# Row maxima turned by VectorE and stored through DRAM, expert gathers spread over steps, a third sum buffer, the first stack loaded in two parts

## The reference, cut to what matters

```python
scores = jnp.einsum('bhqd,bhkd->bhqk', q, k) * scale + bias   # 16 heads of 16, causal, 2048 x 2048
attn = jax.nn.softmax(scores, axis=-1)
out = jnp.einsum('bhqk,bhkd->bhqd', attn, v)
...
xs = xf[tok]                                   # 1024 tokens, 2 experts of 8 each, sorted by expert
h = gelu(ragged_dot(xs, w1, tokens_per_expert))
out = zeros_like(xf).at[tok].add(ragged_dot(h, w2, tokens_per_expert) * flat_w[order][:, None])
```

## Time and profile before

| | |
|---|---|
| runs, us | 4152.18, 4156.4, 4167.15; median 4156.4 |
| profiled execution: its own time, its span | 4157.57, 4155.8 |
| TensorE matmul busy | 3989.5 us, 96% |
| VectorE, ScalarE, GpSimd busy | 2997.2, 2798.6, 846.1 us |
| mean granted TensorE clock | 0.990 |

### The profile page before, as it was taken

One profiled execution on the slowest core, in us unless ns is written; L12 is line 12 of the kernel. 1 busy time (PEld: TensorE's weight loads), 2 busy tenths in 40 slices (PEclk: granted clock), 3 DMA queues, 4 the chain that ended last, 5 costly groups with the idle time before them and its releaser, 6 DMA issues.

```text
span 4155.8 us, 108094 instructions
## 1 busy us (share of the span) xinstructions
PE 3989.5 (96%) x42400; PEld 2460.7 (59%) x42401; DVE 2997.2 (72%) x4046; ACT 2798.6 (67%) x5828; POOL 846.1 (20%) x1176
## 2 busy tenths in 40 slices
PE   6999999999999999999999999999999999999998
PEld 4555555555555555557865555555555555558854
DVE  5888888887878788873038888888888878881074
ACT  2677777777777777775247777777777777773264
POOL 3100001111111123231022333333323232110020
PEclk8999999999999999999999999999999999999999
DMA  6322233324333343235553333333333333345522
GB/s 182 76 57 54 61 82 79 70 75 88 81 77 78 84 104 104 81 102 172 178 156 84 93 91 90 94 98 98 98 91 96 86 77 87 68 103 191 181 71 71
DMA packets 246892, 406.29 MB, mean 98 GB/s; under 512 B 29307, under 2 KB 161859, under 8 KB 233283
## 3 DMA queue, kind: packets, MB, share of 16 engines
q1 hardware_dynamic: 243310, 390.99, 35.8%
q0 software_dynamic: 3072, 8.39, 0.8%
HBM read 263.78 MB, written 121.21 MB: 93 GB/s over the span
## 4 chain that ended last, share of the span: by engine, by line
PE 48%; ACT 4%; DVE 3%; issue 2%; DMA 1%; SPq 0%; ACTq 0%; POOL 0%; DVEq 0%
PE ps_acc L1027 12%; PE ps_r L966 9%; PE ps_p L996 8%; PE ps_p L1137 5%; PE ps_r L1150 5%; ACT probs L848 4%; PE ps_r L1065 3%; DVE part_max L1326 2%; PE ps_r L1073 2%; PE ps_r L1069 1%; PE ps_r L971 1%; PE ps_p L990 1%; PE ps_p L1003 0%; PE ps_r L962 0%; PE ps_r L1058 0%
## 5 line engine op out<-in xcount | busy, mean ns | idle before, releaser
L1326 DVE TENSOR_REDUCE part_max<-ps_p 128x2 f32<-128x1024 f32 (+3 forms) x2560 | 2625.5, 1061 | 654.4 <-PE ps_p L996 496.4
L848 ACT ACTIVATE probs<-ps_r 128x512 f32<-128x512 f32 (+1 forms) x4608 | 2335.2, 575 | 667.0 <-PE ps_r L966 402.2
L966 PE MATMUL ps_r<-q_stack,k_stack 54*128 54x512 f32 (+3 forms) x5120 | 1381.3, 392 | 31.4 <-ACT probs L848 27.9
L996 PE MATMUL ps_p<-k_stack,q_stack 52*128 52x512 f32 (+3 forms) x5120 | 1238.2, 425 | 49.9 <-DVE part_max L1326 25.3
L1027 PE MATMUL ps_acc<-probs,v_head 128*17 128x256 f32 x19456 | 1146.1, 361 | 1.6 <-ACT probs L848 1.6
L966 PEld LDWEIGHTS ps_r<-q_stack,k_stack 54*128 54x128 f32 x5120 | 727.3, 187 | 261.7 <-ACT probs L848 212.7
L1027 PEld LDWEIGHTS ps_acc<-probs,v_head 128*17 128x17 f32 x19456 | 488.8, 97 | 463.0 <-issue 224.1
L996 PEld LDWEIGHTS ps_p<-k_stack,q_stack 52*128 52x128 f32 x5120 | 556.6, 186 | 343.3 <-issue 161.4
L1401 DVE COPY xf<-ps_r 128x256 f32<-128x256 f32 x60 | 25.5, 425 | 402.3 <-PE ps_r L1150 402.3
L911 ACT ACTIVATE hid_f<-ps_p 128x256 f32<-128x256 f32 x240 | 92.0, 383 | 301.7 <-PE ps_p L1137 301.7
L971 PE MATMUL ps_r<-id,mk 64*128 64x64 bf16 x3558 | 280.6, 194 | 0.0
(11 more groups left out here) (134 smaller groups left out, 2408.0 us busy)
## 6 DMA issues: line engine op xcount, KB each, us to landing
probs<-w_dram SPq DMA_DIRECT2D x58, 1024.0 KB, 7.1
q_stack<-parts SPq DMA_DIRECT2D x384, 128.0 KB
k_stack<-parts SPq DMA_DIRECT2D x384, 128.0 KB
parts<-pa SPq DMA_DIRECT2D x128, 256.0 KB, 2.5
parts<-pb SPq DMA_DIRECT2D x128, 256.0 KB, 3.5
o_sums<-acc_sb SPq DMA_DIRECT2D x1008, 17.0 KB
swp<-tmp SPq DMA_DIRECT2D x128, 128.0 KB
bk<-recips SPq DMA_DIRECT2D x58, 256.0 KB
```

The lines of the kernel that those rows point to most:

```text
L848: act.activation(probs[:, at % PBUF, u, 0:w], block_bank(g, n, u)[:, 0:w], ACT.Exp)\
L966: mm = pe.matmul(bank[:, col:col + QW - q0], ks[s][r, kb * P:(kb + 1) * P], qs[s][r, qt * QW + q0:(qt + 1) * QW], start=fresh, stop=True, ...
L996: mm[u] = pe.matmul(banks[:, u, col:col + w], qs[s][r, qb * P:(qb + 1) * P], ks[s][r, kc * QW:kc * QW + w], start=fresh, stop=True, skip_g ...
L1326: mm = dve.tensor_reduce(part_max[:, :, qb, kc], ps_p[:, p1_banks(g, n), col:col + w], AX_X, ALU.max)
```

## The change

1. `c` is no job of TensorE and ScalarE any more. VectorE itself transposes `cp` in blocks of 32 x 32 to `cblk`; SP stores that to DRAM (`cd`, steps 26 and 4) and loads it back, rearranged in runs of 32 numbers, into `q_stack` (`c`, steps 29 and 7).
2. `acc_sb` has three buffers in place of two.
3. The 16 gathers of an expert stage stand at steps 3, 5, 7 and so on of the next stack; the mixing starts at step 31 in place of 19.
4. Stack 0 is loaded in two parts, chunks 0 to 2 while chunk 3 is still computed; SP waits for `rows_copied` only after the first chunk's stores, and the constant rows of slots 1 and 2 come after stack 0.
5. ScalarE ends each expert stage with an exponential of one column, which loads that table there.
6. `bl` of a chunk stands 20 steps ahead of the projection in place of 16, but not before 16 steps behind the last projection of a routed chunk (2 behind another).
7. `zx` stands 5 steps behind its load `zr` in place of beside it.

```diff
-C_HI, C_LO = 28, 4
+C_HI, C_LO = 29, 7
...
+        free = 16
         for c in range(NQ):
...
+            out += [(max(y_at[0] - 20, free), ("bl", r, c, 0)), (y_at[0] - 10, ("bm", r, c, 0))]
             done = y_at[CH - 1] + 3
-            out += [(y_at[0] - 16, ("bl", r, c, 0)), (y_at[0] - 10, ("bm", r, c, 0))]
+            free = done + (16 if routed(r, c) else 2)
...
+            at = GATHER_STEP + 2 * i
+            if g == EX_AFTER[ly] + 1 + at // STEPS:
+                steps[at % STEPS].append(("fg", ly, 0, i))
...
-            steps[n] += [("zr", LAST, c, 0), ("zx", LAST, c, 0)]
+            steps[n].append(("zr", LAST, c, 0))
+            steps[n + 5].append(("zx", LAST, c, 0))
...
-RING_JOBS = ("xt", "qk", "v", "y", "c")
+RING_JOBS = ("xt", "qk", "v", "y")
...
+            def load_first_stack(chunks):
+
+                c = chunks.stop - 1
+                for i in range(2):
+                    sp.wait_ge(parts_st[i], 32 * (c + 1))
+                cols = slice(chunks.start * QW, chunks.stop * QW)
+                for k in range(6):
+                    stack, first, src = stack_piece(0, k)
+                    load_rows(stack[:, cols], first, src[:, cols], stack_in[0])
...
+                elif kind == "cd":
+                    sp.wait_ge(c_ready, 2 * f + (1 if c else 2))
+                    if f:
+                        sp.wait_ge(rows_in[c], 32 * f)
+                    sp.dma_start(c_d[c], cblk[c][:, :]).then_inc(c_st[c], 16)
                 elif kind == "c":
-                    sp.wait_ge(ring_used, PLACE[(kind, f, c, i)] + 1)
+                    sp.wait_ge(c_st[c], 16 * (f + 1))
+                    src = c_d[c].rearrange("(b u i t) n -> u i t b n", b=4, u=2, i=2)
...
             for j in AHEAD:
                 job(*j)
+                if j == ("st", 0, 0, 1):
+                    sp.wait_ge(rows_copied, 16)
+                    load_constant_rows(0)
+                    for k in range(6, stack_loads(0)):
+                        load_stack(0, k)
+                elif j == ("st", 0, NQ - 2, 1):
+                    load_first_stack(slice(0, NQ - 1))
+            load_first_stack(slice(NQ - 1, NQ))
...
+                act.activation(warm[:, :], identf[:, 0:1], ACT.Exp)
...
-                    dve.tensor_tensor(b, negmax[:, :, cols], a.bitcast(F32), ALU.subtract).then_inc(c_ready, 1)
+                    dve.tensor_tensor(b, negmax[:, :, cols], a.bitcast(F32), ALU.subtract).then_inc(c_second, 1)
+                    dve.wait_ge(c_second, nth + 1)
+                    if g:
+                        dve.wait_ge(c_st[int(hi)], 16 * g)
+                    dve.transpose(cblk[int(hi)][:, :], cp[:, int(hi), :, :, :].bitcast(F32).rearrange("p u i t -> p (u i t)"))\
+                        .then_inc(c_ready, 1)
```

More of the change, by code:

```diff
@@ L43 @@
 PBUF = 8
+ACCS = 3
 CH = 4
@@ L194, in jobs_of @@
                 steps[at % STEPS].append(("fm", ly, 0, i))
-    if g == EX_AFTER[0] + 2:
-        steps[STEPS - 1].append(("fo", 0, 0, 0))
+        for i in range(TOPK * NFT):
+            at = GATHER_STEP + 2 * i
+            if g == EX_AFTER[ly] + 1 + at // STEPS:
+                steps[at % STEPS].append(("fg", ly, 0, i))
+    if g == EX_AFTER[0] + 3:
+        steps[24].append(("fo", 0, 0, 0))
     if g == EX_AFTER[0] or g == EX_AFTER[1]:
@@ L254, in ring_uses @@
 def ring_uses():
[L256 removed]
+    seq = [j for j in BEFORE if j[0] in RING_JOBS]
     for g in range(NG):
@@ L268, in stack_count @@
 def stack_count(g):
-    return 32 * (3 + sum(stack_loads(k) for k in range(g % SLOTS, g + 1, SLOTS)))
+    split = 6 if g % SLOTS == 0 else 0
+    return 32 * (3 + split + sum(stack_loads(k) for k in range(g % SLOTS, g + 1, SLOTS)))
 def build(nc, x_in, w_a, wo_a, bqk_a, bv_a, bo_a, w_b, wo_b, tri_in, ramp_in, cos_t, sin_t, rows_in_t,
@@ L280, in build @@
     r_d = nc.dram_tensor("recips", (2, H, L), F32, kind="Internal").ap()
+    c_d = nc.dram_tensor("maxima", (2, P, 4 * TT // 2), F32, kind="Internal").ap()
     rows_d = nc.dram_tensor("rows_copy", (T_ROWS, L), F32, kind="Internal").ap()
@@ L321, in build @@
         cp = sb("cp", [P, 2, 2, 2, TT // 2], F32R)
-        crow = [sb(f"crow{i}", [4 * TT // 2, P], F32R) for i in range(2)]
+        cblk = [sb(f"cblk{i}", [P, 4 * TT // 2]) for i in range(2)]
         stats = sb("stats", [P, 2, CH, 6])
@@ L396, in build @@
         rows_in = [sem(f"rows_in{i}") for i in range(2)]
-        o_st = [sem(f"o_st{i}") for i in range(2)]
+        o_st = [sem(f"o_st{i}") for i in range(ACCS)]
         l_in = sem("l_in")
@@ L419, in build @@
         c_first = sem("c_first")
+        c_second = sem("c_second")
+        c_st = [sem(f"c_st{i}") for i in range(2)]
         c_ready = sem("c_ready")
@@ L539, in load_stack @@
                 if k < 6:
[L540 to L543, removed]
+                    stack, first, src = stack_piece(g, k)
+                    load_rows(stack, first, src, stack_in[s])
                 elif beta >= B:
@@ L614, in job @@
                 elif kind == "zl":
-                    for j in range(2):
-                        sp.wait_ge(o_st[j], 64 * NQ * (NG - 1) // 2)
+                    for j in range(ACCS):
+                        sp.wait_ge(o_st[j], 64 * stores_of(j, NQ * (NG - 1)))
                     src = o_d[f % 2, 0:EARLY, DH, :].rearrange("h (a n) -> h a n", n=D)
@@ L708, in store_mixed, with load_constant_rows @@
                 sp.dma_start(to, xb[:, :, :]).then_inc(ffn_stored, 16)
-            sp.wait_ge(rows_copied, 16)
-            for s in range(SLOTS):
+            def load_constant_rows(s):
                 load_rows(qs[s], POS + 2, table(T_POS, 2), stack_in[s])
@@ L716, in _ @@
                 job(*j)
-            for g in range(2):
-                for k in range(stack_loads(g)):
-                    load_stack(g, k)
+                if j == ("st", 0, 0, 1):
[6 more added lines that the diff above has]
+            load_first_stack(slice(NQ - 1, NQ))
+            load_constant_rows(1)
+            load_constant_rows(2)
+            for k in range(stack_loads(1)):
+                load_stack(1, k)
             zero = rows_in_t[T_ZERO:T_ZERO + 1, :]
@@ L724, in _ @@
                 job(*j)
+            job("cd", 0, 1, 0)
             job("c", 0, 1, 0)
@@ L804, in job @@
                     pool.tensor_tensor(rows, rows, bias[:, :], ALU.add).then_inc(res_out, 1)
+                elif kind == "fg":
+                    gather(f, i)
                 elif kind == "fs":
@@ L918, in _ @@
                 job(*j)
-            job("c", 0, 1, 0)
             for g in range(NG):
@@ L1049, in job @@
                     pe.wait_ge(wo_in, 16 * (ly + 1))
-                elif kind == "c":
-                    pe.wait_ge(c_ready, 2 * f + (1 if c else 2))
                 if at >= RING:
```

64 lines of the change are left out of this document (32 added, 32 removed), and 2 rows, old and new, of the table LAST_JOBS.

## The result

The changed kernel took 4093.7 us in the median of four runs (4087.5 to 4099.2), against 4154.3 for the kernel before (four runs, 4149.0 to 4167.2). The ratio is 0.9849, with a 95% interval of 0.9827 to 0.9872. Faster by some 61 us, where 90.5 were forecast; 4093.7 lies at the upper edge of the range. The profiled execution took 4098.6, with a span of 4096.8.

A forecast was written before the change was run, and what follows sets the result against it. TensorE, busy 96%, was taken as the bound. The terms -68 + 4 + 1 - 14 - 5 - 2.5 - 2 - 4 sum to -90.5 us, so 4067 from the profiled 4157.6, or 4066 beside the median; range 4044 to 4094.

The forecast's parts named there:

- Maxima, -68: Steps 4 and 28: taking the maxima's transpose off TensorE saves 68 us, bounds 31.9 to 69.7.
- +1: First stack's rows: one more DMA landing, less the transpose and ScalarE's copy that go, adds 1 us.
- 0.58 and 0.68 us for each `c` with a job: Saving per `c` beside another job: 58 at step 4, 53 at step 28, 69.7 us in all.
- The 16 that stand alone: The `c` at steps 4 and 28 without another job beside them: taken to gain 0.
- Rival A: Maxima: the bank wait is not their own, so part 1 brings 32 us instead of 68; 4102 us, chance 0.12.
- VectorE's side, +4: Some 10 of 128 places where a norm follows the maxima: 0.3 to 0.7 us each, +4 with clock, 0 to 25.
- Rival B: VectorE's longer chain turns 1.2 us waits into 1.9 and the clock falls: 25 us at six places, 4090; chance 0.13.
- The 10 us of slack: Upper half's maxima rows: in through DRAM by 1114 to 1115, wanted at the next stack's step 0 at 1124.8.
- step 0 never waiting for `maxima`: Sign of being right: at a stack's step 0 no wait for the maxima's rows coming through DRAM.
- Start, -14: Start: unit 0 begins at about 54 us instead of 68.1, saving 14 us; bounds -16 to -8.
- rival D: Start: stores and loads hinder each other, nothing gained, 4080 us; sign: unit 0 after 60; chance 0.08.
- Gathers, table, `bl`, `zx`, -13.5: Stalls removed: gathers behind first stage -5, exponential table -2.5, loads (stack 29) -2, `zx` (stack 62) -4 us.

The follow-up runs named there:

- run 3: Changed kernel with the maxima's rows transposed by TensorE and copied by ScalarE again, without the way through DRAM: 4208.2 us, ratio 0.9979 to the kernel before.
- run 5: The changed kernel itself timed once more, nothing altered: 4093.2 us, ratio 0.9843 to the kernel before.
- run 9: Changed kernel with only the zero fill of rows_by_expert moved to stack 1, step 12: 4080.9 us, ratio 0.9813 to the kernel before.
- run 4: Changed kernel with VectorE's block transpose done twice in each of the 128 places: 4159.2 us, ratio 0.9864 to the kernel before.
- run 8: Changed kernel with late zero fill, norms' pieces two steps away from the maxima, routed norm's pieces every three steps: 4130.3 us, ratio 0.9931 to the kernel before.
- Run 2: Changed kernel with only the zero fill of rows_by_expert moved to stack 1, step 12: 4146.9 us, ratio 0.9831 to the kernel before.
- run 7: Changed kernel with gathers, exponential table, `bl`, `zx` and `fo` as before; VectorE's transposes, new start and three sum buffers stay: 4108.4 us, ratio 0.9879.
- run 12: Kernel before with only VectorE's transpose of the maxima, their rows through DRAM, and the third sum buffer: 4118.2 us, ratio 0.9905 to the kernel before.
- runs 1 to 4: The first four follow-up runs, each a variant of the changed kernel, beside which the kernel before took 4215.3 us.
- runs 5 to 12: The other eight follow-up runs, beside which the kernel before took 4157.4 us (next four) and 4157.7 us (last four).
- run 6: Changed kernel with the later chunks' norm pieces right behind the maxima (steps 27 and 35) moved two steps later: 4095.9 us, ratio 0.9847 to the kernel before.

## Why the prediction was right and where it was not

Faster was forecast and faster came, but a third of the 90.5 us is missing, and 4093.7 lies within the range by 0.3 us. That is luck as much as merit: another set of runs can move the median by that much. The main mechanism was right; one term came to nothing and one cost was three to five times what was taken.

**Maxima, -68, with +4 and +1.** Right in mechanism. The size is 61 to 63 us by the medians, before new stalls are taken off, and 53.5 in the whole by run 3; alone, 39. The mis-sized term is 0.58 and 0.68 us for each `c` with a job, 69.7 in all: it measured some 58, since the `xt` cycles gave 0.27 and most others at step 28 about 0.6. The 16 that stand alone, taken at 0, gave 5 to 6. Rival A was right for the 21 `xt` cycles and wrong for the others.

**VectorE's side, +4.** 0.27 us was taken and 0.21 plus a wait of 0.035 measured; places with a norm behind the maxima did stall, and the cycles more than 0.25 us over the median of their kind, in stacks 1 to 25 and 34 to 61, hold 32.6 us in all after the change, against 12.6 before (33.9 in run 5, 25.1 in run 9). So the new stalls cost 12 to 21 us with the clock's part, where 4 was taken and 25 was the upper bound. How much of this is VectorE's stays open: run 4 can't tell, and some is SP's. Rival B was partly true; its sum, 4066 + 25, is 4091 and not 4090. What the prediction did not see is that one of the worst stalls (where stack 13 begins) is SP's: it asked what is "queued behind SP's new wait", not what the new DMAs are queued behind, and so took part 1 and part 6 as independent. The 10 us of slack were used up twice in the changed kernel's first trace and four times in run 5's, against the sign "step 0 never waiting for `maxima`", and in run 8 overrun by 10.

**Start, -14.** The step that failed. Unit 0 at 54 was 4 us too early (58.3), and above all the sum ended there: that units which begin sooner end sooner was not worked out. They met the zeros' transfer, which had been harmless, and the gain was 0 instead of 14. It was rival D's result, though by another transfer than it named, and without its sign: unit 0 came well before 60. Runs 2 and 9 show the cause by taking it away.

**Gathers, table, `bl`, `zx`, -13.5.** 15 us by run 7, give or take 12. `zx` was worth more than 4: stack 62 is 7.2 us shorter than before, and 9.4 shorter in run 5's trace than in run 7's. Against this, the moved `bl` costs something where it meets the maxima's rows.

**Sum.** -53.5 - 15 + 0 = -68.5 by single runs, or -54 with the 39 of run 12; -61 measured, and -64 in run 5. The terms have intervals of 10 to 12 us either way and the whole one of 9, so they agree no closer than this.

## What to carry to other kernels

When work is made to begin earlier, list the bulk transfers that had been hidden beside it and ask what each now stands in front of: the rebuilt start gave nothing until one other DMA was moved. A row that takes a new way through one engine's DMA queue depends on everything ahead of it there, its conditional waits and long issues included; check the worst place, not the typical slack, and check it in the job table as the whole change leaves it, since another part may have put something in front. And a stall that is removed at one step is only gained if the stall behind it was not already waiting.

## Of the hardware, unexpected

- On the chip of runs 1 to 4 all kernels took about 60 us more, and the traces put this where GpSimd issues indirect DMAs. Run 2 there against run 9 elsewhere (the same kernel): stacks 26 to 30 take 297.4 against 287.2 us, 32 and 33 together 123.5 against 109.7, 56 to 59 227.4 against 208.7, and 61 70.2 against 53.1. ScalarE and VectorE both stop while GpSimd ends its burst. Run 2, timelines of POOL, DVE and ACT:

```profile
1619.96 0.97 POOL L865 DMA_INDIRECT rows_by_expert<-xf,slot_of  x1 [0.30 <-issue]
...
1622.30 1.23 DVE L1366 TENSOR_REDUCE part_max<-ps_p 128x2 f32<-128x1024 f32 x1 [4.68 <-remote]
...
1622.25 1.08 ACT L898 ACTIVATE probs<-ps_r 128x512 f32<-128x512 f32 x2 [4.23 <-remote]
```

  "remote" stands for a release that the profile puts down to no instruction. The four traces of this chip have such waits; the kernel before's, the changed kernel's first and the eight of runs 5 to 12 have none. Why one chip does this stays open; a gain of ten microseconds can only be read beside the kernel before on the same chip.
- SP's issue of a DMA is not of fixed length. Of the changed kernel's 252 groups of four stores of sums most take 1.4 us to issue; 26 take 2.3 to 7.1, nearly all directly behind other DMAs (the loads of a `bl` or of a stack, or an `sw`). The kernel before has 26 such groups too, of up to 6.8 us. Why the issue is held isn't shown.
- The 16 KB store of the maxima lands after 4.0 us in the median in run 6 (3.3 in run 7), not after the 2.5 of the earlier trace rows. The Trainium skill, DMA: Bandwidth & Descriptors, § Specifications, has transfers under 512 B read, modified and written. Packets under 512 B rose from 29307 to 64314, but no run here varied their size, so its part in this isn't shown.
